# Two gated cross-attention layers with expert networks on one core: the accumulations of expert e ahead of the gathers of expert e+2 in GpSimd's list

## The reference

```python
def _L1_ffn_ref(x, Wr, W1, b1, W2, b2):
    xt = x.reshape(N, D)                       # N = 4096, D = 128
    scores = jax.nn.softmax(xt @ Wr, axis=-1)
    G, idx = jax.lax.top_k(scores.T, k)        # k = 1024 tokens for each of 8 experts
    X_in = xt[idx]
    h = gelu(einsum('ekd,edh->ekh', X_in, W1) + b1)    # hidden width 512
    X_e = einsum('ekh,ehd->ekd', h, W2) + b2
    contrib = (G[..., None] * X_e).reshape(E * k, D)
    out = jnp.zeros((N, D)).at[idx.reshape(-1)].add(contrib)
```

## Time and profile before

| | us |
|---|---|
| median of 3 runs | 1138.19 |
| lowest, highest | 1134.05, 1138.41 |
| profiled execution | 1138.09 |
| its span | 1136.4 |
| TensorE busy (matmul) | 851.7 |
| DVE busy | 666.6 |
| GpSimd busy | 567.9 |
| ScalarE busy | 535.5 |

### The profile page before, as it was taken

One profiled execution on the slowest core, in us unless ns is written; L12 is line 12 of the kernel. 1 busy time (PEld: TensorE's weight loads), 2 busy tenths in 40 slices (PEclk: granted clock), 3 DMA queues, 4 the chain that ended last, 5 costly groups with the idle time before them and its releaser, 6 DMA issues. The chain is left out here.

```text
span 1136.4 us, 30955 instructions
## 1 busy us (share of the span) xinstructions
PE 851.7 (75%) x9978; PEld 623.5 (55%) x9978; DVE 666.6 (59%) x2230; ACT 535.5 (47%) x1782; POOL 567.9 (50%) x952
## 2 busy tenths in 40 slices
PE   0899999999994388818999999999811279766670
PEld 0677677767773166605777777777510147554460
DVE  2367777777775933314778888888667854321110
ACT  0477766666773012205777777777600034222220
POOL 4223333333321257547776777776100067777776
PEclk9999999999996699958999999999955579888885
DMA  4101111111111134222222222221000114333333
GB/s 125 56 35 64 65 63 62 62 62 62 62 58 58 49 86 116 57 67 58 62 71 72 69 69 69 69 69 38 16 20 0 43 44 81 62 60 63 62 33 28
DMA packets 64374, 67.27 MB, mean 59 GB/s; under 512 B 23934, under 2 KB 50924, under 8 KB 64290
## 3 DMA queue, kind: packets, MB, share of 16 engines
q1 hardware_dynamic: 50466, 56.53, 16.1%
q0 software_dynamic: 13824, 9.66, 6.4%
HBM read 44.06 MB, written 27.39 MB: 63 GB/s over the span
## 5 line engine op out<-in xcount | busy, mean ns | idle before, releaser
L534 ACT ACTIVATE P<-bank,mx 128x120 f32<-128x120 f32 x1024 | 282.7, 397 | 0.6
L703 DVE TENSOR_REDUCE mx<-bank 128x4 f32<-128x480 f32 x256 | 153.3, 651 | 75.0 <-PE bank L424 74.9
L437 PE MATMUL bank<-ident,P 128*120 128x128 f32 x1024 | 162.0, 281 | 6.3 <-ACT P L534 4.3
L598 POOL TENSOR_SCALAR rs<-mv 128x1 f32<-128x1 f32 x128 | 27.8, 217 | 230.2 <-DVE mv L685 229.6
L437 PEld LDWEIGHTS bank<-ident,P 128*120 128x120 f32 x1024 | 115.5, 142 | 38.5 <-issue 24.0
L1467 POOL DMA_INDIRECT out<-y,add_token x64 | 102.6, 1603 | 23.4 <-issue 21.9
L424 PEld LDWEIGHTS bank<-Kf,Qm 32*128 32x128 f32 x2048 | 95.1, 188 | 32.7 <-issue 32.7
L424 PE MATMUL bank<-Kf,Qm 32*128 32x120 f32 x2048 | 113.0, 284 | 0.0
L453 PE MATMUL bank<-PT,Vb 120*32 120x128 f32 x2048 | 106.5, 280 | 0.1
L453 PE MATMUL bank<-PT,headcols 120*32 120x128 f32 x2048 | 103.4, 274 | 0.0
L414 PE MATMUL bank<-bp,identb 128*128 128x480 bf16 x384 | 99.9, 371 | 0.0
(11 more groups left out here) (219 smaller groups left out, 1804.5 us busy)
## 6 DMA issues: line engine op xcount, KB each, us to landing
choice_rows<-zeros SPq DMA_DIRECT2D x32, 384.0 KB, 2.4
yrows<-choice_rows SPq DMA_DIRECT2D x32, 384.0 KB, 3.1
w<-in_w13T SPq DMA_DIRECT2D x8, 704.0 KB, 4.1
token_rows<-payload SPq DMA_DIRECT2D x32, 128.0 KB, 1.7
ctx<-in_ctxT SPq DMA_DIRECT2D x64, 60.0 KB, 2.4
w<-in_w2T SPq DMA_DIRECT2D x8, 352.0 KB
token_rows<-payload SPq DMA_DIRECT2D x32, 68.0 KB, 1.6
X<-in_x SPq DMA_DIRECT2D x8, 256.0 KB
```

Source lines behind the costliest of these rows:

```text
L437: mm = nc.tensor.transpose(TB[r % 2][0:KV, S * j:S * j + S], t.P[:, r, j, :], t.ident[:])
L534: e = nc.scalar.activation(t.P[:, r, j, :], heads(SC[r])[:, j, :], ACT.Exp, bias=t.mx[:, G * r + j:G * r + j + 1], scale=-1.0)
L703: ve.tensor_reduce(t.mx[:, G * r:G * r + G], heads(SC[r]), AX.X, ALU.min).then_inc(ev.mins, 1)
```

## The change

In GpSimd's list of the second experts, the body for expert e had the gathers for expert e+2 and then the accumulations of expert e. Now it has them the other way round.

```diff
@@ -1473,9 +1473,9 @@
                 gather(e + 1, 1 - u)
 
             def body(e, u):
+                add(e, u)
                 if exists(e + 2):
                     gather(e + 2, u)
-                add(e, u)
 
             experts(pool, ahead, body)
```

## The result

The changed kernel takes 1145.72 us (median of five, 1144.98 to 1149.27) where the kernel before takes 1138.11 in the same series; the ratio is 1.0084, with a 95% interval of 1.0059 to 1.0109, or 7 to 12 us. It is slower, as forecast, but by 7.6 us in the medians and 9.6 by the ratio, where 16 was forecast. The median lies 1.3 us under the range of 1147 to 1163; the ratio, applied to the 1138.19 of the kernel before, gives 1147.8, at its low end. The profiled execution took 1148.83 us with a span of 1147.1, 10.7 over the span before, against the 16.3 that the sum gave. It is one of two longer ones of its five (1148.83 and 1149.27; the other three are 1144.98 to 1145.72), 3.1 over their median, while the profiled one of before was at its median.

The account below looks back on a forecast made before the run. GpSimd's instruction list was taken to bound the second experts; 14.4 + 19.0 - 17.9 + 0.8 = +16.3 us on a span of 1136.4 gave 1152.7, plus 1.69 to the execution time: 1154 us, range 1147 to 1163.

Parts of the forecast that it names:

- What bounds the kernel, and the wait inside each accumulation: GpSimd's list bounds the second experts; the fifth accumulation of experts 1 to 6 waits 2.4 us each, +14.4 us.
- release and restart: From DVE's scale end to GpSimd's waiting accumulation: 0.07 us for release plus 0.55 for restart.
- a0 in front: Expert 0's accumulations now precede expert 2's gathers, whose list copy comes at 951.6 instead of 932.60: +19.0 us.
- One group less at the end: Behind the six gather-and-accumulate pairs only expert 7's accumulations remain, not expert 6's too: -17.9 us.
- a7's new wait: Expert 7's accumulations, now nearer to its gathers, wait for the scale of its first half: +0.8 us.
- ... as an accumulation runs beside them in both orders, it is no term.: DVE's L1492 and L1493 cost a GpSimd instruction 0.4 us, in both orders, so nothing was added.
- at the same 27.13 apiece without the stalls: Six gather-and-accumulate pairs on GpSimd keep their former 27.13 us each, apart from the new waits.
- DVE holds the restart off: Rival, 0.07: experts 1 to 3's fifth accumulation loses DVE's whole 2.03 us pair, +4.9 us, giving 1159.
- From the span to the median: Profiled execution took 1.69 us over its span and lay 0.1 under the median, so no further correction was made.
- No stall at full clock: Rival, 0.08: TensorE at full clock readies the scale before GpSimd arrives, delay under about 8.2 us; 1139.
- Lower clock for longer: Rival, 0.12: TensorE at 0.5 clock throughout adds 1.5 us per expert, six stalls grow by 9.0; 1163.
- Catching up: Rival, 0.03: accumulations after a wait run 0.6 us shorter as the queue empties, giving back 19.2; 1135.

Follow-up runs that it names:

- out_first_after: Changed kernel with TensorE doing the second half of out of expert e ahead of the transposes of expert e+1; 1139.3 us, ratio 1.0025 to the kernel before.
- more_out_after: Changed kernel with 16 needless TensorE transposes ahead of the second half of out; ratio 1.0224 to the kernel before.
- kept_warm: Changed kernel with 64 needless transposes (110 ahead of expert 2's) in TensorE's idle time before each expert's transposes from expert 2 on; 1144.7 us, ratio 1.0064 to before.
- kept_warm_longer: As kept_warm, with 90 (102 for the last three) needless transposes instead of 64; ratio 1.0175 to the kernel before.

## Why the prediction was right in kind and too large in size

- *What bounds the kernel, and the wait inside each accumulation.* Right. Six waits, each at the fifth accumulation, 13.2 us where 14.4 was said (10.8 to 17.4). out_first_after shows the cause and more_out_after the price of one for one. Inside it two pieces missed in opposite directions. The delays were 9.08 to 10.60, 9.96 in the mean, not 10.3: I had looked for the clock of longer idle times and found clocks of 0.59 to 0.76. (The "about 9 us" of idle time before each expert's transposes held for experts 4 to 7 only; it was 6.4 ahead of expert 3's, and ahead of those of 1 and 2 there was none.) And release and restart together are 0.76 to 0.77 in all six (1002.23 - 1001.46), not 0.62: a DMA behind a wait starts as a DMA behind its list copy does.
- *a0 in front.* 18.6 where 19.0 was said (950.72 - 904.96 against 932.60 - 905.45).
- *One group less at the end.* The distance of the last two copies in the profile before, -17.9, needed no guess. The copy of a7 again waits 1.9 us for landed accumulations; the one of a6 doesn't. With a0 in front that makes 0.7 us, so nearly all of the change's cost is the six waits.
- *a7's new wait.* 0.6 where 0.8 was said: the copy-to-DMA time is 1.52 instead of 0.94.
- *"... as an accumulation runs beside them in both orders, it is no term."* This is the step that failed, together with "at the same 27.13 apiece without the stalls". The six pairs without their waits took (1123.75 - 950.72 - 13.2) / 6 = 26.6 us apiece, 2.9 less in all. The 96 DMAs of these pairs were 3.8 us shorter together (121.6 us instead of 125.4), and 0.9 came back, as the copy for expert 2's gathers now stands directly behind accumulations and has 1.89 us to the first gather instead of 0.96. In the order before, eleven DMAs of the pairs began while L1492, L1493 or L1524 ran, and eight of them lost 0.2 to 0.8 us, the last of a0 the most:

```profile
958.42 1.28 DVE L1493 SCALAR_TENSOR_TENSOR oh<-slotno,lasts,oh 128x1024 bf16<-128x1024 f32 x1
...
958.77 2.36 POOL L1467 DMA_INDIRECT out<-y,add_token  x1 [0.30 <-issue]
```

  In the new order five began so and lost 0.03 to 0.14. GpSimd stands idle while L1524 of the second half runs, and restarts 0.76 us behind it: for experts 1 to 3 L1492 has then 0.2 us left, and L1493 ends inside the fifth accumulation; behind experts 4 to 6 there is no further list to find. So the wait that the change makes shelters GpSimd from DVE; in out_first_after, without the waits, the DMAs are 5.0 us longer again. I had the rows for this (1.96 at 1010.00) and the Trainium skill's rule, and treated both as a price on the restart that could only be added. The rival "DVE holds the restart off", +4.9, had the wrong sign.
- The rest of the sum: the stage began 0.5 us earlier, and from the last DMA to the end it was 0.3 less. 13.2 + 18.6 - 2.9 - 17.9 + 0.6 - 0.5 - 0.3 = 10.8, and the spans differ by 10.7.
- *From the span to the median.* I took one profiled execution for the median. That of before was; that of the changed kernel lay 3.1 us above its own. This is as large as the failed step; without it the median would have been in the range. The low end, 1147, was the sum's small ends and 3 us; it held neither a gain from DVE nor a spread of the executions.
- *No stall at full clock* was given 0.08, with a delay of about 8.2 us as the limit and so a clock over 0.9. It did not come about in the changed kernel. The mechanism was right (6.06 us at full clock, and the wait that went in kept_warm), but the limit was too loose: with 0.76 for release and restart a wait begins at a delay of 7.8, and full clock gives 7.7. *Lower clock for longer* is refuted: idle times of 10.3 to 13.8 us gave delays of 9.1 to 10.6, no longer than idle times of 9 us had given. *Catching up* is refuted as well: the accumulation behind each wait takes 1.55 to 1.59.

## What to carry to other kernels

When the engine that bounds a stage issues both the input of step e+1 and the output of step e, work for step e that is queued behind something waiting for the input of e+1 turns an order that only looks tighter into a wait in every round. Move that work ahead of the waiting instruction before closing up the bounding engine's list. Where two engines hinder each other, a new wait shifts when they meet, so the hindrance of before is a term with a sign of its own, not a constant.

## What the runs showed of the hardware beyond what was expected

A GpSimd DMA that begins while one of DVE's L1492, L1493 or L1524 runs is held until about 0.13 us before that ends: up to 0.8 us each, some 6 us over the second experts before, 4 of them in the six pairs. The first GpSimd DMA behind a semaphore from DVE starts 0.76 us after the end of DVE's row, six times within 0.01 (0.86 and 0.79 ahead of a0 and a7), against 0.30 between two of its DMAs in a row. TensorE at the lower level after more than 10 us of idle time took the same 1.97 us for eight transposes as after 9, and as after 3.48 in kept_warm; with work added while the clock was low, the work behind it ran faster (3.74 us instead of up to 5.78). Small matmuls in a row, with nothing to wait for, did not always run back to back: in kept_warm_longer gaps of 0.2 to 1.2 us lay in the runs of 90 and 102, and one of 0.6 in its run of 110, while the 110 in kept_warm ran 12.19 us without one. Why was not found.
